# Moving a step's first half of score matmuls ahead of the two matmuls that feed the max reduction, in a fused token-mixing and attention kernel

## The reference, cut to what matters

```python
q, k, v = (shp(q), shp(k), shp(v))
attn = jax.nn.softmax(jnp.einsum('bhsd,bhtd->bhst', q, k), axis=-1)
ctx = jnp.einsum('bhst,bhtd->bhsd', attn, v)
...
x = x + _L0_attn_ref(xn, ...) + _L0_ffn_ref(xn, ...)
```

## Time and profile before

| | |
|---|---|
| median of 3 runs | 485.09 us (484.5 to 487.07) |
| the profiled execution, its own time | 488.56 us |
| its span, first to last instruction | 486.8 us |
| mean granted TensorE clock | 0.979 |
| PE busy, share of the span | 443.1 us, 91% |
| DVE busy | 380.5 us, 78% |
| ACT busy | 357.3 us, 73% |
| one iteration of 32 steps | 97.9 us |

### The profile page before, as it was taken

One profiled execution on the slowest core, in us unless ns is written; L12 is line 12 of the kernel. 1 busy time (PEld: TensorE's weight loads), 2 busy tenths in 40 slices (PEclk: granted clock), 3 DMA queues, 4 the chain that ended last, 5 costly groups with the idle time before them and its releaser, 6 DMA issues.

```text
span 486.8 us, 8478 instructions
## 1 busy us (share of the span) xinstructions
PE 443.1 (91%) x3204; PEld 143.6 (29%) x3206; DVE 380.5 (78%) x678; ACT 357.3 (73%) x477; POOL 176.9 (36%) x223
## 2 busy tenths in 40 slices
PE   2988998999999999999999999999999999999993
PEld 1734323222223322222222222222222222222252
DVE  8667748899988779999887799998877999960033
ACT  3244676679988747799787477997874779979852
POOL 4032891213842332128323321283333212843300
PEclk9988998899999999999999999999999999999997
DMA  6004200213222313142223131413231302010314
GB/s 226 3 7 57 30 6 9 26 22 57 34 45 47 32 24 56 19 59 34 44 42 38 25 53 19 62 23 55 28 52 23 53 14 47 1 34 18 93 36 159
DMA packets 46332, 20.82 MB, mean 43 GB/s; under 512 B 37460, under 2 KB 37588, under 8 KB 46292
## 3 DMA queue, kind: packets, MB, share of 16 engines
q1 hardware_dynamic: 45472, 19.61, 23.8%
q10 hardware_dynamic: 820, 0.68, 0.4%
HBM read 4.88 MB, written 5.24 MB: 21 GB/s over the span
## 4 chain that ended last, share of the span: by engine, by line
PE 58%; DVE 24%; ACT 12%; DMA 2%; issue 2%; POOL 1%; SPq 0%; DVEq 0%
PE banks L1396 17%; DVE neg_half L1114 16%; PE banks L1385 13%; PE banks L1311 11%; PE banks L1357 8%; ACT probs L906 8%; DVE run L1067 3%; PE banks L1275 2%; PE banks L1208 2%; PE banks L1165 1%; ACT work L865 1%; POOL work L600 1%; DMA parts<-ctx_dram 1%; PE banks L1266 1%; ACT work L863 1%
## 5 line engine op out<-in xcount | busy, mean ns | idle before, releaser
L1114 DVE TENSOR_REDUCE neg_half<-banks 128x1 f32<-128x512 f32 x512 | 319.9, 683 | 37.5 <-PE banks L1311 36.2
L906 ACT ACTIVATE probs<-banks 128x1024 f32<-128x1024 f32 x256 | 247.8, 1022 | 63.9 <-PE banks L1385 61.2
L1396 PE MATMUL banks<-probs,v_op 128*32 128x512 f32 x1024 | 137.0, 607 | 0.4 <-ACT probs L906 0.4
L1311 PE MATMUL banks<-k_main,q_main 64*128 64x512 bf16 x512 | 121.5, 389 | 13.9 <-DVE neg_half L1114 12.2
L1385 PE MATMUL banks<-q_main,k_main 64*128 64x512 bf16 x512 | 101.1, 382 | 4.9 <-ACT probs L906 3.7
L1385 PE MATMUL banks<-q_tail,k_tail 35*128 35x512 bf16 x512 | 100.9, 381 | 0.0
L1311 PEld LDWEIGHTS banks<-k_main,q_main 64*128 64x128 bf16 x512 | 36.3, 94 | 167.5 <-DVE neg_half L1114 143.9
L1385 PEld LDWEIGHTS banks<-q_main,k_main 64*128 64x128 bf16 x512 | 26.0, 95 | 44.5 <-ACT probs L906 32.1
L1385 PEld LDWEIGHTS banks<-q_tail,k_tail 35*128 35x128 bf16 x512 | 26.6, 95 | 23.5 <-issue 0.5
L1090 DVE TENSOR_TENSOR rec<-banks,quarter_in 128x512 f32<-128x512 f32 x4 | 2.8, 692 | 37.8 <-PE banks L1357 37.8
L702 POOL TENSOR_TENSOR work<-work 128x512 f32<-128x512 f32 x12 | 12.5, 1042 | 49.7 <-ACT work L891 49.7
(11 more groups left out here) (173 smaller groups left out, 439.3 us busy)
## 6 DMA issues: line engine op xcount, KB each, us to landing
ctx_dram<-ctx_sb SPq DMA_DIRECT2D x16, 256.0 KB, 2.0
q_main<-parts SPq DMA_DIRECT2D x60, 48.0 KB
k_main<-parts SPq DMA_DIRECT2D x60, 48.0 KB
parts<-ctx_dram SPq DMA_DIRECT2D x8, 256.0 KB, 4.1
mat_sb<-in_mats_dram SPq DMA_DIRECT2D x2, 768.0 KB, 5.3
q_tail<-max_parts SPq DMA_DIRECT2D x96, 2.0 KB
v_op<-V SPq DMA_DIRECT2D x16, 64.0 KB, 3.6
out_dram<-x_sb SPq DMA_DIRECT2D x4, 256.0 KB, 3.0
```

The costliest lines, as they stand in the source:

```text
L906: a.activation(probs[:, (2 * step + h) % 4, :, :], banks[:, 2 * h:2 * h + 2, :], ACT.Exp).then_inc(b_read, 1)
L1114: v.tensor_reduce(neg_half[:, s, u:u + 1], src, axis=AX.X, op=ALU.max, negate=True).then_inc(a_read, 1)
L1311: mm(dst, q_main[HALF * e:HALF * (e + 1), s, P * c:P * c + P], k_main[HALF * e:HALF * (e + 1), s, CHUNK * h:CHUNK * h + CHUNK], start=True ...
L1396: last = mm(banks[g:g + 32, PV_BANK, :], v_op[:, s % 2, step, e, :], probs[:, (2 * step + h) % 4, e, :], start=(step == 0), stop=(step == ...
```

## The change

PE's steps begin with B0 instead of with the two A scores of the first list; those two now stand between B0 and B1. Nothing else is changed: the same instructions, banks and counts.

```diff
                 t = j * KEY_TILES + step
                 todo = place_turns[t]
-                for turn in todo[0]:
-                    fill_turn(it, turn)
                 if step == 0:
                     pe.wait_ge(tail_in[p % 2], (p // 2 + 1) * 64)
                     pe.wait_ge(max_in[j % 2], (it * 2 + j // 2 + 1) * 32 * PARTS)
                 scores(p, j, step, 0)
+                for turn in todo[0]:
+                    fill_turn(it, turn)
                 scores(p, j, step, 1)
                 for turn in todo[1]:
                     fill_turn(it, turn)
```

## The result

| | before | changed |
|---|---|---|
| median | 485.83 us (4 runs) | 518.73 us (4 runs, 517.62 to 519.58) |
| profiled execution | 488.56 us, span 486.8 | 519.58 us, span 517.9 |
| mean granted clock | 0.979 | 0.981 |

The ratio is 1.0676 (95% interval 1.0635 to 1.0717): 32.9 us slower, where 36.5 were forecast. The time is 518.73 us against a forecast of 521.6 and a range of 510 to 528.

The account below looks back on a forecast made before the run. A PE-DVE loop (V, A0, DVE's reading, A3, V) was taken to bound the plain step. Terms 23.5 + 8.3 + 2.2 + 1.7 + 0.8 = 36.5 us on 485.1 gave 521.6 us, range 510 to 528.

Parts of the forecast that it names:

- loop over two engines: Step without product: V to A0, DVE's reading of A0, A3, then V again, together 2.49 us.
- Plain and product gaps: V-to-V times without or behind a product: 0.44 us more each, to 2.93 and 3.78; terms 23.5 and 8.3 us.
- transpose gaps: Steps with the transpose, t = 4 and 20: 3.10 to 3.41 us, +0.31; seven gaps, 2.2 us.
- Scan gaps: t = 3 and 7, set by DVE's scan pair behind its reads: stay at 3.67 us, no cost.
- the last product: Step behind it, t = 30: DVE's subtraction and 1.05 us of sums hide B0, no cost.
- t = 11 to 13: Three gaps where ACT's exponentials and branch are last, 9.84 us together: +0.1 us taken.
- the mean step: Step behind the mean product, t = 18: DVE's 0.69 us subtraction lets A0 come 0.44 later unseen, no cost.
- rival 1: Gaps next to DVE- or ACT-bound ones pass on their lead; a third of 31.8 us gone, 511 us; chance 0.10.
- The term of the first steps: Start of the kernel, half of it near the 1.2 GHz clock: between 0 and 2 us, 0.8 us taken.
- Rival 2: DVE has unread banks enough and sets 2.4 us a step, so order doesn't matter: 485 us; chance 0.04.
- rival 3: ACT gets B0 earlier; gaps at t = 11 to 13 fall, 3 us in all, 482 us; chance 0.02.
- Rival 4: Added PE idle makes its clock fall; a fifth of 115 steps affected, +32 us, 553 us; chance 0.04.

Follow-up runs that it names:

- experiment 3: Kernel before, with only the two main matmuls of B0 ahead of A0 and A1 in all steps: 498.59 us, ratio 1.0244.
- experiment 4: Kernel before, with B0 and B1 both ahead of all four A scores: 561.37 us, ratio 1.1538.
- experiment 5: Kernel before, with B1 moved between A3 and V, A0 directly behind V: 524.29 us, ratio 1.0788.
- experiment 6: Changed kernel, with DVE's maximum over only the first 256 columns of an A bank: 479.70 us, ratio 0.9877 to the kernel before.
- experiment 7: Kernel before, with DVE's maximum over only half of each A bank's columns: 466.74 us, ratio 0.9615.
- experiment 10: Kernel before, with B0 ahead of A0 and A1 only in t = 8, 9 and 10: 487.71 us, ratio 1.0020.
- experiment 1: Kernel before, with B0 ahead of A0 and A1 only in t = 3, 7, 13, 18 and 30: 487.14 us, ratio 1.0029.
- experiment 2: Kernel before, with B0 ahead of A0 and A1 only in the 15 steps of 2.49 us per iteration: 505.06 us, ratio 1.0377.
- experiment 8: Kernel before, with V ahead of the transpose in t = 4, 12, 20 and 28: 485.85 us, ratio 1.0005.
- experiment 9: Kernel before, with the product of t = 29 issued in t = 30 between A1 and B0: 484.61 us, ratio 0.9971.
- experiment 11: Kernel before, with the products of t = 29 and t = 17 each issued one step later between A1 and B0: 483.59 us, ratio 0.9938.

## Why the prediction was right

**The bound.** That the plain step is a loop over two engines, and not PE's or DVE's rate, is shown by four things: the chain of the changed kernel, the doses of experiments 3 and 4, experiment 5 with the same price at the other end of A3, and experiments 6 and 7, which change DVE's part alone. Experiment 7 gives the size of the cover that was left: 0.08 us. The chain view of the kernel before could not have shown it: between 224.96 and 231 us it runs through PE alone, and the short wait of A3 does not appear in it. That wait was seen only in the starts of A2 and A3.

**The terms.** Plain and product gaps came out at 2.92 and 3.78, to 0.01 us of the forecast, and so did transpose gaps with 3.41. Scan gaps and the last product cost nothing, as said.

**What was mis-sized.** From the first V to the last the time rose by 33.6 us; my terms for that stretch sum to 35.7. An iteration rose by 9.93 us, where they sum to 10.3. The difference is in two terms. For t = 11 to 13 I took +0.1 and it was -0.12, since ACT's lag of experiment 10 is not paid any more. For the mean step I took nothing and it was -0.09. The latter is two effects. The order in that step costs 0.12 (experiment 1), so that DVE's subtraction hides 0.32 of the 0.44 and not all of it. And longer steps ahead of it take back 0.21 (3.87 to 3.65 in experiment 2), by a wait that I had not looked at. The mean product reads what POOL makes last (`x1_ready`). Before:

```profile
229.82 1.28 POOL L678 TENSOR_TENSOR work<-hT,quarter_in 128x512 f32<-128x512 f32 x1
231.25 1.07 PE L1357 MATMUL banks<-work,mean_w 128*32 128x512 f32 x8
```

Changed:

```profile
239.10 1.27 POOL L678 TENSOR_TENSOR work<-hT,quarter_in 128x512 f32<-128x512 f32 x1
242.32 1.04 PE L1357 MATMUL banks<-work,mean_w 128*32 128x512 f32 x8
```

Before, POOL ends at 231.10, and the product starts 0.15 later and 1.09 behind its V (230.16). In the changed kernel POOL has ended 1.95 us ahead, and the product starts 0.88 behind V (241.44), as in experiment 2: 0.21 less. In rival 1 I had named a return and given it the wrong place: the plain gaps keep their full price beside long ones, and it is the long ones that shrink. The last iteration rose by 4.9, and 0.43 of its shortfall is t = 20, where the first gap without A scores went from 2.62 to 2.19.

The term of the first steps was wrong in sign: +0.8 taken, and the first V of the profile came 2.6 us earlier (86.50 before, 83.90 now). The granted clock differs there. Windows of the kernel before:

```profile
80.00:84.00 4.00, 3.28 (x15) 1.60 (x17) 2.84 (x6) 1.94 (x2) 0.00 (x0) 0.62 0.06 8
84.00:88.00 4.00, 4.00 (x19) 0.81 (x15) 2.86 (x5) 1.94 (x2) 0.00 (x0) 0.53 0.45 52
```

And of the changed kernel:

```profile
80.00:84.00 4.00, 3.47 (x26) 1.11 (x27) 3.71 (x7) 3.61 (x4) 0.00 (x0) 1.00 0.25 32
84.00:88.00 4.00, 3.87 (x30) 0.92 (x32) 3.56 (x7) 2.20 (x3) 0.00 (x0) 1.00 0.59 58
```

The granted clock was about half in one execution and full in the other. The profiles of experiments 1, 8 and 10 have the low clock there too, those of 2 to 7, 9 and 11 have not. From the first B matmul to the first V it takes 4.7 and 5.7 us in experiments 1 and 8 and 3.7 to 4.7 in 2 to 5. So the first steps in the order of the kernel before were seen with either clock (low in four profiles, full in three), the orders with matmuls moved in these steps only with the full one (six profiles, that of the changed kernel among them). Whether an order favours one of the two was not settled; it is a matter of 1 to 2 us. Since the four iterations alone add 33.6 us and the medians differ by 32.9, the start gave back no more than a microsecond on average.

**Rivals.** Rival 2 (the order does not matter) and rival 3 (ACT is fed earlier) fell: ACT got B0 ahead of the A scores and waited 17 us longer all the same. Rival 4 did not occur: PE stands still for a fraction of a microsecond in each plain step, and the granted clock is 1.00 over the whole iteration. In the other profiles it fell after the first steps, while A scores ran, only in experiment 5, twice, at a cost of 1.1 us each time. The Trainium skill's rule in "TensorE: Matmul & The Clock Gate", section "A second HAM failure mode: psum-queue depth-cycling", is not borne out by the trace of the changed kernel, though its banks are cycled and PE pauses in each plain step.

## What to carry to other kernels

Before moving an instruction on a busy engine, find the loop that sets the step: the matmul that waits for a bank, the reading that frees it, and the matmul that was read. In this kernel work between the filling and the refilling of the same bank was free until it outlasted the reading; everything on the other side was paid in full wherever no other engine was last, so the longest pieces belong inside. Where another engine is behind over several steps, both gains and losses of single steps come back partly in the next ones, so sum over the stretch, not the step.

## What the runs showed of the hardware

A matmul of 512 columns that a DVE reduction reads costs the loop 0.42 us from its start to the reduction's start, 0.69 for the reduction of 512 columns (0.42 for 256), and 0.06 from its end to the start of the matmul that waited. V, whose tiles have another shape, starts 0.32 us after a lone A3 (227.36 to 227.68), where B pairs follow each other at 0.22. What I had not expected is how close the two came: the loop takes 2.49 us a plain step and PE alone 2.41, so PE at 91% busy looked like the bound and was not. In experiment 5 the granted clock fell after a pause of PE of 1.21 us in two of three like places, and the gap that followed took 1.1 us more.
